# Transposed-score attentions: key chunks split a step later, maxima turned before the sums, scores waiting chunk by chunk

## What is computed

```python
# L0_xattn: 8 heads of 64, keys are the normalised context and the 64 latents themselves
xn = layernorm(x, ln_x_g, ln_x_b)
ln = layernorm(latents, ln_l_g, ln_l_b)
kv_in = jnp.concatenate([xn, ln], axis=1)
...
sim = jnp.where(full_mask[:, None, None, :], sim, max_neg)
attn = jax.nn.softmax(sim.astype(jnp.float32), axis=-1).astype(sim.dtype)
out = jnp.einsum('bhij,bhjd->bhid', attn, v)
...
# L1_xattn: 16 heads of 64, keys are the plain context
sim = jnp.einsum('bhnd,bhmd->bhnm', q, k) * d ** (-0.5)
attn = jax.nn.softmax(sim, axis=-1)
out = jnp.einsum('bhnm,bhmd->bhnd', attn, v)
```

## Time and profile before

| | |
|---|---|
| median of 3 runs | 3221.08 us (3220.84 to 3226.75) |
| the profiled execution's own time | 3231.05 us |
| its span, first to last instruction | 3229.3 us |
| mean granted TensorE clock | 0.907 of full |
| TensorE busy, matmuls | 2705.7 us (84%) |
| VectorE busy | 1829.2 us (57%) |
| ScalarE busy | 1578.5 us (49%) |
| GpSimd busy | 1319.2 us (41%) |

### The profile page before, as it was taken

How to read it: one execution, slowest core, us unless ns; L and a number is a source line. 1 busy time by engine, 2 the same in 40 slices (tenths; PEclk the granted TensorE clock), 3 DMA queues, 4 the chain that set the end, 5 groups by cost and what they waited for, 6 DMA issues and landing times. The chain is left out here.

```text
span 3229.3 us, 44186 instructions
## 1 busy us (share of the span) xinstructions
PE 2705.7 (84%) x15983; PEld 2112.0 (65%) x15983; DVE 1829.2 (57%) x3672; ACT 1578.5 (49%) x2758; POOL 1319.2 (41%) x994
## 2 busy tenths in 40 slices
PE   5788888635789999999996779496899999999777
PEld 4678878513578888888886456365466666666546
DVE  6676666463364544454443344613778778777462
ACT  3666666211265655565563224232555555555332
POOL 0665665230056566665561016001454454454130
PEclk7899999757899999999998889798999999999975
DMA  3232231021201101011100123112000000000000
GB/s 98 63 94 63 67 89 42 16 28 40 67 21 31 42 22 42 21 42 31 31 11 5 40 65 102 25 43 59 21 22 11 21 21 11 21 21 1 22 1 14
DMA packets 238573, 120.11 MB, mean 37 GB/s; under 512 B 37784, under 2 KB 233024, under 8 KB 238400
## 3 DMA queue, kind: packets, MB, share of 16 engines
q1 hardware_dynamic: 238400, 117.81, 13.7%
HBM read 101.46 MB, written 15.28 MB: 36 GB/s over the span
## 5 line engine op out<-in xcount | busy, mean ns | idle before, releaser
L703 POOL TENSOR_TENSOR L_xattn_held<-L_xattn_held,L_xattn_shift 128x512 f32<-128x512 f32 (+1 forms) x613 | 761.5, 1284 | 621.6 <-ACT L_xattn_shift L632 621.6
L446 PEld LDWEIGHTS L_xattn_acc<-L_xattn_rows,L_xattn_held 128*128 128x128 f32 (+2 forms) x5120 | 642.0, 200 | 68.4 <-DVE L_xattn_mixed L787 36.3
L446 PE MATMUL L_xattn_acc<-L_xattn_rows,L_xattn_held 128*128 128x129 f32 (+2 forms) x5120 | 654.2, 284 | 26.9 <-DVE L_xattn_mixed L787 17.8
L1387 POOL TENSOR_TENSOR L_xattn_projected<-L_xattn_along,L_xattn_crossed 128x512 f32<-128x512 f32 (+1 forms) x256 | 271.4, 1068 | 383.0 <-DVE L_xattn_crossed L1428 383.0
L613 ACT ACTIVATE L_xattn_held<-L_xattn_held 128x512 f32<-128x512 f32 (+2 forms) x640 | 401.6, 631 | 0.3
L606 ACT COPY L_xattn_held<-L_xattn_ring 128x512 f32<-128x512 f32 (+1 forms) x416 | 242.8, 584 | 275.5 <-DVE L_xattn_running L806 259.5
L806 DVE TENSOR_TENSOR L_xattn_running<-L_xattn_ring,L_xattn_running 128x512 f32<-128x512 f32 (+1 forms) x384 | 264.3, 688 | 116.3 <-PE L_xattn_ring L430 98.7
L428 PE MATMUL L_xattn_ring<-L_xattn_queries_hi,L_xattn_keys_hi 128*128 128x512 f32 (+2 forms) x640 | 285.0, 445 | 38.6 <-DVE L_xattn_keys_lo L734 35.5
L430 PE MATMUL L_xattn_ring<-L_xattn_queries_hi,L_xattn_keys_lo 128*128 128x512 f32 (+2 forms) x640 | 256.9, 401 | 0.0
L429 PE MATMUL L_xattn_ring<-L_xattn_queries_lo,L_xattn_keys_hi 128*128 128x512 f32 (+2 forms) x640 | 256.4, 401 | 0.0
L1292 ACT COPY L_xattn_probT<-L_xattn_bank_a 128x512 f32<-128x512 f32 (+2 forms) x320 | 138.9, 454 | 221.4 <-PE L_xattn_bank_a L1124 221.4
(11 more groups left out here) (491 smaller groups left out, 4447.2 us busy)
## 6 DMA issues: line engine op xcount, KB each, us to landing
L_xattn_raw<-in_ctx SPq DMA_DIRECT2D x16, 768.0 KB
context_normalised<-L_xattn_fresh SPq DMA_DIRECT2D x16, 768.0 KB
L_xattn_rows<-context_normalised SPq DMA_DIRECT2D x16, 768.0 KB
L_xattn_fresh<-in_ctx SPq DMA_DIRECT2D x16, 768.0 KB
L_xattn_rows<-in_ctx SPq DMA_DIRECT2D x16, 768.0 KB
L_xattn_staged<-in_ctx SPq DMA_DIRECT2D x16, 768.0 KB
L_xattn_xhat<-context_normalised SPq DMA_DIRECT2D x16, 768.0 KB
L_ffn_w<-in_L_ffn_W SPq DMA_DIRECT2D x1, 2048.0 KB, 8.9
```

The source lines that it names most:

```text
L446: mm = nc.tensor.matmul(acc[:, c // 2, c % 2 * WIDE:(c % 2 + 1) * WIDE], held[0:n, u % 2, k, c * P:(c + 1) * P], rows[0:n, b % 2, k, :], s ...
L703: nc.gpsimd.tensor_tensor(tile, tile, shift[0:keys_of_tile[k]], ALU.subtract).then_inc(shifted, 1)
L1387: nc.gpsimd.tensor_tensor(projected[:, t % 2, c0:c0 + n], along[:, c0:c0 + n], crossed[:, c0:c0 + n], ALU.add)\
```

## The change

It changes no operation and no size; it moves operations in the program order of TensorE, ScalarE and VectorE and moves waits.

- Jobs are put by step. `mixed` is turned at step 0 (it was step 1), the output product stands at step 2 alone (in L1 now in the other unit of the batch), queries at steps 1 and 2 of units that have no output product, and the four context chunks at the last four steps of a unit (they stood at tiles 6, 8, 10 and 12; in L1 that is steps 3 to 6 before and now, in L0 steps 3 to 6 before and 4 to 7 now).
- VectorE handles the job of a step one step later, after it has seen that step's tiles. ScalarE still rounds in the job's own step.
- TensorE turns the maxima after tile 0's scores and ahead of the sums of step 0; it turned them after these sums. It turns them back ahead of step 2's sums (it was after step 1's), and ScalarE keeps them at the start of step 3.
- A unit that begins a batch no longer waits for all jobs before it; tiles 0, 4, 8 and 12 each wait for their own chunk.
- In L0, measuring is spread over all steps, two tiles a step; moments are gathered at step 2, the root is taken there on ScalarE, and normalised rows are written at steps 3 to 6.
- `mixedT` and `moments` get two buffers.

```diff
-    LATER = 6
+    LATER = 7
@@ jobs_of(u): keyed by step n now, not by tile k @@
         if 3 <= u <= UNITS + 2:
-            jobs[1] = ("mixed", (u - 3) % NG, (u - 3) // NG % 2)
-        if NG == 2 and g == 0 and b % 2 == 1 and 3 <= b <= BATCHES + 1:
-            jobs[3] = ("output", (b - 3) // 2)
+            jobs[0] = ("mixed", (u - 3) % NG, (u - 3) // NG)
+        if NG == 2 and b % 2 == 1 and 3 <= b and g == (b < BATCHES + 1):
+            jobs[2] = ("output", (b - 3) // 2)
         if NG == 1 and b % 2 == 0 and 4 <= b <= BATCHES + 2:
-            jobs[3] = ("output", (b - 4) // 2)
-        if b + 1 < BATCHES:
-            if g == 0:
-                for c, slot in enumerate((6, 8, 10, 12)):
-                    jobs[slot] = ("context", c)
-            if b % 2 == 1:
-                for q in range(2):
-                    jobs[(4, 5)[q] if g == 0 else (5, 9)[q]] = ("queries", 2 * g + q)
+            jobs[2] = ("output", (b - 4) // 2)
+        if b // 2 + 1 < BATCHES // 2 and b % 2 == 2 - NG:
+            for q in range(2):
+                jobs[1 + q] = ("queries", b // 2 + 1, 2 * g + q)
+        if b + 1 < BATCHES and g == 0:
+            for c in range(len(CTX_CHUNKS)):
+                jobs[len(STEPS) - len(CTX_CHUNKS) + c] = ("context", b + 1, c)
...
+    XHAT_STEP = len(STEPS) - len(CTX_CHUNKS) - 1
@@ block.tensor, score_tile(u, k) @@
+                if g == 0 and k % TURNS == 0 and k < CT:
+                    pe.wait_ge(spare_free, CHUNK_DONE[b, k // TURNS])
@@ block.tensor, unit(u) @@
-                if u < UNITS and u % NG == 0:
-                    pe.wait_ge(spare_free, lane.count())
                 for n in range(max(len(STEPS), len(SUMMED) + 1)):
...
-                    if n < len(SUMMED) and 2 <= u < UNITS + 2:
-                        for k in SUMMED[n]:
-                            sum_tile(u - 2, k)
                     if n == 0 and 1 <= u <= UNITS:
                         pe.wait_ge(tile_seen, u * KT)
...
-                    if n == 1 and 1 <= u <= UNITS:
+                    if n == 2 and 1 <= u <= UNITS:
                         pe.wait_ge(peak_ready, u)
...
+                    if n < len(SUMMED) and 2 <= u < UNITS + 2:
+                        for k in SUMMED[n]:
+                            sum_tile(u - 2, k)
+                    job = JOBS[u].get(n)
@@ block.scalar, unit(u) @@
+                for n, step in enumerate(STEPS):
+                    if n == 3 and 1 <= u <= UNITS:
+                        act.wait_ge(shift_full, u)
...
+                        nc.scalar.copy(shift[:], turned_bank[:]).then_inc(shift_kept, 1)
...
+                    if normed and n == XHAT_STEP - 1 and u + 1 < BATCHES:
+                        context_root(u + 1)
@@ block.vector, beside(u, n, job) and unit(u, job) @@
-                if k == 0 and 1 <= u <= UNITS:
+                if n == 1 and 1 <= u <= UNITS:
                     dve.wait_ge(peaks_turned, u)
...
+                if u + 1 < BATCHES:
+                    if n == XHAT_STEP - 1:
+                        gather_moments(u + 1)
+                    if n == XHAT_STEP:
...
+                    if XHAT_STEP <= n < XHAT_STEP + len(CTX_CHUNKS):
+                        make_xhat(u + 1, n - XHAT_STEP)
+                if u + 2 < BATCHES:
+                    measure(u + 2, range(STEPS[n][0], min(STEPS[n][-1] + 1, CT)))
...
-                    for k in step:
-                        beside(u, k)
+                    beside(u, n, job)
+                    job = JOBS[u].get(n)
```

More of the change, by code:

```diff
@@ L178, in column_attention_stage @@
     JOBS = [jobs_of(u) for u in range(UNITS + 3)]
-    JOBS_BEFORE = [FIRST_JOBS + sum(len(j) for j in JOBS[:u]) for u in range(UNITS + 4)]
-    SPLITS_BEFORE = [FIRST_JOBS + sum(sum(what[0] in ("context", "queries") for what in j.values()) for j in JOBS[:u])
-                     for u in range(UNITS + 4)]
+    CHUNK_DONE = {(0, c): FIRST_JOBS for c in range(len(CTX_CHUNKS))}
+    JOBS_IN_ORDER = [jobs[n] for jobs in JOBS for n in sorted(jobs)]
+    for number, job in enumerate(JOBS_IN_ORDER):
+        if job[0] == "context":
+            CHUNK_DONE[job[1:]] = FIRST_JOBS + number + 1
+    XHAT_STEP = len(STEPS) - len(CTX_CHUNKS) - 1
     with ExitStack() as ctx, ExitStack() as before_batches:
@@ L205, in column_attention_stage @@
         rinv = s.sb("rinv", [P, 2, 2])
-        mixed, mixedT = s.sb("mixed", [P, TURNS, D]), s.sb("mixedT", [P, NH, 2, SEQ])
+        mixed, mixedT = s.sb("mixed", [P, TURNS, D]), s.sb("mixedT", [P, 2, NH, 2, SEQ])
         outT, out_bias = s.sb("outT", [P, TOKENS]), s.sb("out_bias", [P, 1])
@@ L408, in turn_mixed, with output @@
                 filled(turn)
-            def output():
+            def output(pair):
                 bank = fill()
                 for h in range(NH):
-                    mm = nc.tensor.matmul(bank[:, 0:P], fold_vo[:, h, :], mixedT[:, h].rearrange("p b i -> p (b i)"),
+                    mm = nc.tensor.matmul(bank[:, 0:P], fold_vo[:, h, :], mixedT[:, pair % 2, h].rearrange("p b i -> p (b i)"),
                                           start=(h == 0), stop=(h == NH - 1))
@@ L815, in beside @@
                     nc.vector.tensor_copy(peak_wide[:], over_last(peak[:], P)).then_inc(peak_ready, 1)
-                if normed and u + 1 < BATCHES:
-                    if k == 4:
+                if job is not None:
+                    if job[0] == "mixed":
+                        dve.wait_ge(spare_full, lane.count() + 1)
+                        of_g, of = job[1], job[2]
+                        emptied(nc.vector.tensor_copy(mixedT[:, of // 2 % 2, HALF * of_g:HALF * (of_g + 1), of % 2, :],
+                                                      spare[:].rearrange("p (h i) -> p h i", i=SEQ)))
+                    elif job[0] == "output":
+                        lane.next()
+                    elif job[0] == "context":
+                        split_context(job[1], job[2])
+                    else:
+                        split_queries(job[1], job[2])
+                if not normed:
+                    return
+                if u + 1 < BATCHES:
+                    if n == XHAT_STEP - 1:
+                        gather_moments(u + 1)
+                    if n == XHAT_STEP:
                         invert_std(u + 1)
@@ L853, in unit @@
                             see_tile(u, k)
-                    for k in step:
-                        beside(u, k)
-                    if n == 2 and u == UNITS:
+                    beside(u, n, job)
+                    job = JOBS[u].get(n)
+                    if n == 3 and u == UNITS:
                         dve.wait_ge(shift_kept, UNITS)
@@ L864, in _ @@
                 measure(0, range(CT))
-                gather_moments()
+                gather_moments(0)
                 dve.wait_ge(gains_loaded, GAINS)
```

104 lines of the change are left out of this document (35 added, 69 removed).

## The result

The changed kernel takes 3306.88 us (median of 4 runs, 3304.0 to 3311.45) beside 3223.91 us for the kernel before in the same session: ratio 1.0255, 95% interval 1.0233 to 1.0278. That is slower by 83 us. The prediction had the sign, but 3306.88 us lies 39 us above its range; the profiled execution took 3307.61 us, 77 us more than that of before.

A forecast was written before the change was run, and what follows sets the result against it. TensorE's work, its waits and its lowered clock were taken to bound each unit. Terms 19.5 + 17 - 12 - 3 + 1 = +22.5 us (0.70%) gave a median of 3243 us, range 3203 to 3268.

The forecast's parts named there:

- the sign: Whole kernel: slower, +22.5 us on the profiled execution; chance of slower 0.68, faster 0.18, the same 0.14.
- The step that failed: GpSimd's part: 0.6 of its time in use, results needed a unit later, so its cost was taken as nothing.
- the back-turn moved behind two more tiles: End of both stages: the last unit's subtraction starts a little later, +1 us.
- the 15 that the prediction gave it: L0's gain: -12 us from the clock and -3 us in the first two units.
- L0, order: L0 at full clock: old waits go, new chunk and query waits come; sum nothing, within half a microsecond a unit.
- The 3 us given to the first two units: L0's first two units, without sums to hide a wait: -3 us, not worked out.
- L0, clock: L0: idle split into 1.5 and 1.7 us costs less clock, 14 x -0.85 = -12 us; bounds -36 and no difference.
- the prediction's second rival: Clock holds if only gaps of 2.4 us lower it: L1 +19.5, L0 -36 - 3, about -18 us, 3203; chance 0.18.
- L1, order: L1: unit ends and query waits make each four-unit period 2.6 us longer, +19.5 us over 7.5 periods.
- the removed pair: L1: the two query jobs without scores between them go, saving some 2.4 us a period.
- L1, clock: L1: new 2.2 us gaps lower the clock at two of three ends, 1.7 us each, +17 us; bounds 0 and 26.

The follow-up runs named there:

- the scaling first and in pieces: Changed kernel, but GpSimd scales a unit's rows before waiting for the next shift, as 13 one-tile multiplications; ratio 1.0011 to the kernel before.
- the back-turn early: Changed kernel, but in L0 peaks, back-turn and kept shift each stand one step earlier, at steps 0, 1 and 2; ratio 0.9986 to the kernel before.
- the split moved early: Changed kernel, but in L1 the third key chunk is split ahead of the sums' copy and tile 12; ratio 1.0161 to the kernel before.
- the rows scaled twice: Kernel before, but GpSimd multiplies each unit's rows by the gains twice, with a drain ahead; ratio 1.0146 to the kernel before.
- the kernel with the scaling first: Changed kernel, but GpSimd scales a unit's rows in one multiplication before waiting for the next shift; ratio 1.0107 to the kernel before.

## Why the prediction was wrong

**The step that failed** is "GpSimd has 0.6 of its time in use and its results are needed a unit later", costed at nothing. GpSimd's use says how much work it has, not how long its work takes from its release to its user; in the kernel before its results were used 0.2 to 1.1 us after they were written. (In L1's window of the earlier trace rows, too, the prediction names VectorE, at 356.65 us, as the next to matter; ScalarE's 429.85 and GpSimd's 442.38 us are more.) Two kernels show it from both sides: 3.45 us taken out of the loop let L0 end 44.6 us earlier, 3.6 us put into the loop of before cost 47.9 us in 14 units.

The prediction names the edit that lengthened the loop ("the back-turn moved behind two more tiles") and prices it at 1 us, for the last unit alone; even there it was 4.2 us in L0. The loop and its clock make up all of L0's loss: with the scaling first and in pieces L0 ends 16.1 us ahead of before, with the back-turn early, which also ends the queries' waits, 28.5 us ahead. The kernel before with the same scaling in pieces ends L0 at 621.72 us, so that with the loop relieved in both the change is worth 4.8 us in L0, for the 15 that the prediction gave it.

**L0, order.** Gaps of 1.5 and 1.7 us ahead of the chunks and 1.0 ahead of the queries were predicted, 1.75, 1.59 and 0.92 measured. Without the loop an undisturbed unit takes 30.9 us at full clock, where the prediction's "nothing" makes it 34.1 - 2.5 = 31.6; of TensorE's idle in the changed kernel 83.3 - 32.5 = 50.8 us are not the loop's, 0.8 us a unit less than before, for nothing within half a microsecond. The 3 us given to the first two units were not there: from first scores to second turned maxima it is 56.6 us before and 56.9 after.

**L0, clock.** Predicted 12 us back, measured 13.0 us more lost in 14 units. The price was asked of the chunk gaps, but the wait for GpSimd followed 2.6 us behind the second of them. Without that wait the clock held in most units; the prediction's second rival, that gaps of 1.5 and 1.7 us cost none, is then nearly right for L0 (31 us gained to its last result, counted from the first scores, for 39, with the queries' waits gone as well).

**L1, order.** Ends without keys +0.64 us (0.6), ends with keys +0.83 (0.9), the queries' waits 2 x 0.79 = 1.6 (2.0). A period at full clock is 1.73 us longer (2.6), so that the removed pair was worth 2.8 us and not 2.4. This term was 13 us, not 19.5, by the waits and the removed pair in like parts. The prediction calls the window of 714.57 us one of 28 units; it is one of 27, and nothing hangs on it.

**L1, clock.** Two of three gaps of 2.2 us were to be followed by a lower clock, at 1.7 us each. The price was right (108.73 - 107.06 = 1.67 us); the share was not: it was six of 14 (the first of the 15 ends has a gap of 1.48 us only). The changed kernel's second execution has six of 14 as well. The mean of six periods is 108.50 us (1028.37 to 1679.35 us), 1.44 above one at full clock: 11 us over 7.5 periods, where 17 were taken. That the gap does it is shown by the split moved early, which ended it. The Trainium skill (TensorE: Matmul & The Clock Gate, Why this matters for your kernels) names only longer gaps as harmful; those of 2.20 us here did harm in part of the cases.

**L1's two ends** were not worked out. Up to the fourth turned maxima L1 is 3.6 us shorter than before, from there to its last result but for the six periods 8.2 us longer. The first is mostly the copy of the peaks: 5.16 us long at 920.33 in the kernel before, beside GpSimd's subtractions, and 0.68 us after. It was 1.51 us in the run with the old L1 behind the changed L0, whose L1 was 5 us shorter; so it seems to hang on how the stage happens to start, which was not tried. Nor was it tried why the end is longer by as much as 8.2 us.

## What to carry over

Look for loops, not only for the busiest engine: follow each engine's results to their user and back to its own next release, and add up the latencies. A user that starts 0.2 to 0.25 us behind its producer in unit after unit is to be taken as held by it even where no idle time is printed; such a place has no slack for a step that is moved one later. And where the clock of TensorE hangs on its waits, a wait can cost up to twice its length: 38.1 us of idle that went took 36.9 us of busy time along, the 21.3 us that the change brought to 14 L0 units came with 13.0, but the 42.9 us of the rows scaled twice with 5.0 only.

## What the runs showed of the hardware

VectorE's copy of 128x512 elements within SBUF (0.43 us alone) stood for as long as a multiplication of 128x1664 elements was running on GpSimd: 1.93 to 3.51 us in nine units of the kernel with the scaling first. Others stood longer, through instructions that followed each other without a pause: 5.16 us beside subtractions in L1 of the kernel before, 7.37 us beside subtractions and pieces (above), and 8.95 us in the last unit of the changed kernel, beside a subtraction and two multiplications. Each of these twelve ended 0.3 us behind the end of a GpSimd instruction: the nine behind the one that ran when they began, the three behind the last of the row. Operations of VectorE that read TensorE's banks kept their time beside GpSimd's subtractions (0.68 and 0.69 us). The Trainium skill (SBUF — State Buffer, SBUF: two separate sides) describes a pair of ports that VectorE or GpSimd holds for a whole instruction while the other waits. The nine copies and those beside the pieces (at most 0.76 us) agree with that; the three long ones waited for more than one instruction.

In the run with the back-turn early, two gaps of 1.75 and 1.59 us with 1.3 us of work between them left the clock at 1.00 in units of 30.9 us and came with 0.90 and 0.92 in others with the same waits, in one and the same execution (364.70 to 398.90 us and 332.00 to 364.70 us, beside 208.64 to 239.50 us). So a price for the clock per gap is a mean over cases, not a constant.
